# The last norm of a two-layer graph kernel: one-hot rows made on GpSimd by comparison, and one of a batch's four row loads issued by ScalarE

## The reference

```python
x = layernorm(x + gnn_0(x, ...))      # sums over edges, then four dense layers with tanh
x = layernorm(x + gnn_1(x, ...))      # one message of 32 features per edge, added at its destination
# layernorm(v) = (v - mean(v)) / sqrt(var(v) + 1e-5), over the 32 features of a node
```

## Time and profile before

| | |
|---|---|
| median of 3 runs | 1985.52 us |
| lowest, highest | 1982.97, 1986.45 us |
| span of the profiled execution (first to last instruction) | 1707.1 us |
| median less span (time outside the first and last instruction) | 278.4 us |
| VectorE, ScalarE, GpSimd, TensorE busy over the span | 70%, 50%, 63%, 77% |
| the last norm: from 1555.8 us to the last store's issue at 1699.4 us | 143.6 us, 8.4% of the span |
| mean granted TensorE clock over the span | 0.846 |

### The profile page before, as it was taken

One profiled execution on the slowest core, in us unless ns is written; L12 is line 12 of the kernel. 1 busy time (PEld: TensorE's weight loads), 2 busy tenths in 40 slices (PEclk: granted clock), 3 DMA queues, 4 the chain that ended last, 5 costly groups with the idle time before them and its releaser, 6 DMA issues.

```text
span 1707.1 us, 25367 instructions
## 1 busy us (share of the span) xinstructions
PE 1315.9 (77%) x6200; PEld 957.6 (56%) x6200; DVE 1193.5 (70%) x3648; ACT 858.9 (50%) x2256; POOL 1068.9 (63%) x1168
## 2 busy tenths in 40 slices
PE   5699993686513777665778999958999999996673
PEld 1388881242212555554655666635777777775563
DVE  9699995677512443676667999964777777774776
ACT  0167770011101222666775777735666666664884
POOL 7777778777777777774111444448877887830444
PEclk8599996577555999888888999977999999997655
DMA  1000000123224988665555666531222222213785
GB/s 41 13 14 13 14 14 20 47 72 79 67 68 127 257 250 246 171 174 145 132 138 140 179 184 189 163 95 32 58 58 57 58 64 67 59 42 78 196 216 157
DMA packets 298498, 178.98 MB, mean 105 GB/s; under 512 B 28715, under 2 KB 290032, under 8 KB 298352
## 3 DMA queue, kind: packets, MB, share of 16 engines
q1 hardware_dynamic: 219712, 116.54, 26.0%
q0 software_dynamic: 29008, 36.18, 8.3%
q10 hardware_dynamic: 49632, 24.65, 5.0%
HBM read 111.18 MB, written 66.07 MB: 104 GB/s over the span
## 4 chain that ended last, share of the span: by engine, by line
PE 42%; POOL 28%; issue 16%; DVE 8%; DMA 2%; DVEq 2%; SPq 1%; ACT 1%; POOLq 0%; ACTq 0%
PE bank L1025 12%; POOL gat L511 12%; POOL lined L518 11%; PE bank L994 7%; PE bank L1018 7%; DVE res L1308 5%; PE bank L945 3%; POOL out L591 3%; PE bank L947 3%; PE bank L1034 3%; PE bank L1003 3%; PE bank L987 3%; DMA placed<-pay,pos_i 1%; DVEq L1308 1%; DVEq L1302 1%
## 5 line engine op out<-in xcount | busy, mean ns | idle before, releaser
L566 POOL DMA_INDIRECT gat<-x_d,src_i x196 | 253.2, 1292 | 59.0 <-issue 53.1
L511 POOL DMA_INDIRECT gat<-in_x,key_i x196 | 211.1, 1077 | 64.8 <-issue 62.4
L1308 DVE TENSOR_TENSOR res<-res,bank 128x128 f32 x588 | 168.4, 286 | 108.5 <-issue 24.4
L528 POOL DMA_INDIRECT placed<-pay,pos_i x196 | 191.9, 979 | 68.1 <-issue 65.6
L518 POOL DMA_INDIRECT lined<-in_x,other_i x196 | 195.8, 999 | 59.7 <-issue 59.7
L1025 PE MATMUL bank<-prod,ident 128*128 128x280 f32 x896 | 217.0, 400 | 0.0
L1025 PEld LDWEIGHTS bank<-prod,ident 128*128 128x128 f32 x896 | 171.0, 191 | 46.5 <-issue 0.6
L956 PE MATMUL bank<-woh,pw 128*128 128x128 f32 x784 | 135.4, 335 | 69.3 <-DVE woh L1287 33.4
L956 PEld LDWEIGHTS bank<-woh,pw 128*128 128x128 f32 x784 | 120.3, 238 | 85.5 <-DVE woh L1287 44.5
L56 ACT ACTIVATE xt<-bank 128x128 f32<-128x128 f32 x98 | 26.6, 271 | 269.6 <-PE bank L897 261.2
L1018 PE MATMUL bank<-rw,ht 65*128 65x384 f32 x392 | 141.3, 514 | 23.3 <-ACT ht L738 13.8
(11 more groups left out here) (204 smaller groups left out, 2840.5 us busy)
## 6 DMA issues: line engine op xcount, KB each, us to landing
pw<-placed SPq DMA_DIRECT2D x588, 68.0 KB, 2.1
pw<-placed SPq DMA_DIRECT2D x98, 272.0 KB
xin<-in_x_t SPq DMA_DIRECT2D x53, 256.0 KB, 3.2
placed<-pay SPq DMA_DIRECT2D x49, 272.0 KB, 2.4
x_d<-res POOLq DMA_DIRECT2D x49, 256.0 KB, 3.8
placed<-pay SPq DMA_DIRECT2D x28, 448.0 KB, 3.2
out<-out ACTq DMA_DIRECT2D x49, 256.0 KB, 2.7
xin<-in_x_t ACTq DMA_DIRECT2D x45, 256.0 KB, 3.6
```

Source lines behind the costliest of these rows:

```text
L511: pool.indirect_dma_start(gat[:, t, :], None, x, bass.IndirectOffsetOnAxis(ap=key_i[:, 0, t:t + 1], axis=0)).then_inc(s_gat, 16)
L528: pool.indirect_dma_start(placed[1].rearrange("t p r -> (t p) r"), bass.IndirectOffsetOnAxis(ap=pos_i[:, 1, t:t + 1], axis=0), pay[i % 4][ ...
L566: pool.indirect_dma_start(gat1[g % 3][:, k, :], None, x1_d, bass.IndirectOffsetOnAxis(ap=src_i[:, t:t + 1], axis=0)).then_inc(c_gat[g % 3] ...
L1308: add.up(dve.tensor_tensor(into, into, quarter(bank + k // G, k % G), ALU.add))
```

## The change

GpSimd no longer subtracts; it makes the one-hot rows itself, with four `tensor_scalar` instructions per batch on 128x128: (iota + 128 * window) compared for equality with the row's key, the key read from column 128 of the loaded rows as a scalar per partition. Nothing goes over ScalarE any more: `away4`, its semaphore, the four 128x128 and the one 128x512 activation per batch are gone. On GpSimd the step is scale(s - 10), hot(s).

ScalarE's step is store(s - 13), square(s - 7), load(s): it now issues the fourth row load of each batch, with the register load for its tile number, and waits with it as SyncE does (`z_mm`, b - 5). SyncE issues the other three. ScalarE's first load also waits for a new semaphore `z_stored`, which SyncE raises when the stores of stage 3 are done. TensorE's and VectorE's lists are unchanged.

```diff
+BY_SP = 3
...
-        away4 = ring(sb, "away4", 2, [P, G, P])
...
-        def first_rows(sp, to, c, b, landed):
+        def first_rows(eng, on, to, c, b, ks, landed):
             _, tiles = nc.values_load_multi_w_load_instructions(
-                t0_i[0:1, c, G * b:G * b + G], engines=[mybir.EngineType.SP], min_val=0, max_val=NT,
+                t0_i[0:1, c, G * b + ks.start:G * b + ks.stop], engines=[on], min_val=0, max_val=NT,
                 skip_runtime_bounds_check_because=IN_RANGE)
-            for k in range(G):
-                sp.dma_start(to[:, k, :], placed[c][bass.ds(tiles[k], 1)].rearrange("t p r -> p (t r)")).then_inc(landed, 16)
+            for k, tile in zip(ks, tiles):
+                eng.dma_start(to[:, k, :], placed[c][bass.ds(tile, 1)].rearrange("t p r -> p (t r)")).then_inc(landed, 16)
...
             sp.wait_ge(c_mm, NU)
+            sp.sem_inc(z_stored, 1)
             for b in range(NB):
                 wait(sp, z_mm, b - 5)
-                first_rows(sp, pw4[b % 6], 1, b, z_pw[b % 6])
+                first_rows(sp, mybir.EngineType.SP, pw4[b % 6], 1, b, range(BY_SP), z_pw[b % 6])
...
-            def apart_4(b):
+            def hot_4(b):
                 pool.wait_ge(z_pw[b % 6], 16 * G * (b // 6 + 1))
-                wait(pool, z_away, b - 2)
-                pool.tensor_tensor(kr4[b % 3][:, :], w128[:, G * b:G * b + G], pw4[b % 6][:, :, P], ALU.subtract).then_inc(z_kr, 1)
-            staged([apart_4] + [None] * 9 + [scale_4], NB)
+                wait(pool, z_mm, b - 2)
+                for k in range(G):
+                    ins = pool.tensor_scalar(oh4[b % 3][:, k, :], iota[:, 0:P], float(P * (G * b + k)), pw4[b % 6][:, k, P:P + 1],
+                                             ALU.add, ALU.is_equal)
+                ins.then_inc(z_oh, 1)
+            staged([hot_4] + [None] * 9 + [scale_4], NB)
...
             act.wait_ge(c_mm, NU)
-            def away_from_4(b):
-                act.wait_ge(z_kr, b + 1)
-                wait(act, z_oh, b - 1)
-                for k in range(G):
-                    ins = act.activation(away4[b % 2][:, k, :], iota[:, 0:P], ACT.Abs, bias=kr4[b % 3][:, k:k + 1])
-                ins.then_inc(z_away, 1)
-            def hot_4(b):
-                act.wait_ge(z_away, b + 1)
-                wait(act, z_mm, b - 2)
-                act.activation(oh4[b % 3][:, :, :], away4[b % 2][:, :, :], ACT.Relu, bias=1.0, scale=-1.0).then_inc(z_oh, 1)
-            staged([away_from_4, hot_4, None, None, None, square_4] + [None] * 5 + [store_4], NB)
+            act.wait_ge(z_stored, 1)
+            def load_4(b):
+                wait(act, z_mm, b - 5)
+                first_rows(act, mybir.EngineType.Activation, pw4[b % 6], 1, b, range(BY_SP, G), z_pw[b % 6])
+            staged([load_4] + [None] * 6 + [square_4] + [None] * 5 + [store_4], NB)
```

More of the change, by code:

```diff
@@ L291, in gnn_kernel @@
         c_prod, c_sum, c_scal, c_pay, c_mm, c_msg = sem("c_prod"), sem("c_sum"), sem("c_scal"), sem("c_pay"), sem("c_mm"), sem("c_msg")
-        z_pw, z_kr, z_away, z_oh, z_mm = ring(sem, "z_pw", 6), sem("z_kr"), sem("z_away"), sem("z_oh"), sem("z_mm")
+        z_pw, z_kr, z_oh, z_mm, z_stored = ring(sem, "z_pw", 6), sem("z_kr"), sem("z_oh"), sem("z_mm"), sem("z_stored")
         z_y, z_sq, z_ssq, z_root, z_out = sem("z_y"), sem("z_sq"), sem("z_ssq"), sem("z_root"), sem("z_out")
@@ L446, in _ @@
                 freed(sp, b - 5)
-                first_rows(sp, pw[b % 6], 0, b, s_pw[b % 6])
+                first_rows(sp, mybir.EngineType.SP, pw[b % 6], 0, b, range(G), s_pw[b % 6])
             def load_extra(i, c):
@@ L463, in _ @@
                 wait(sp, s_back, min(i - 5 - D_EXTRA, NG))
-                first_rows(sp, pw[i % 6], 1, b, s_pw[i % 6])
+                first_rows(sp, mybir.EngineType.SP, pw[i % 6], 1, b, range(G), s_pw[i % 6])
                 if b >= 5:
```

## The result

The changed kernel takes 2049.5 us (2048.2 to 2053.2) where the one before takes 1986.0: ratio 1.0327, 95% interval 1.0304 to 1.0349, or 63.5 us slower. The prediction was 1995.3 with a range of 1970 to 2034: the right sign, and under a sixth of the size.

The account below looks back on a forecast made before the run. SyncE's loads were taken to bound the last norm at 2.54 us a batch, ScalarE close behind. Start -0.5, first nine intervals -4.1, other 39 +15.3 and tail -0.9 made +9.8 on 1985.5: 1995.3 us, range 1970 to 2034.

Parts of the forecast that it names:

- What binds before: Last norm: SyncE's loads lead at 2.40 us a batch plus hiccups, ScalarE second, 2.28 us busy a batch.
- the 15 us that were to show the forecast: Sign on GpSimd: its waits for loaded rows fall from 98.8 us to under 15.
- The comparison on GpSimd: GpSimd, last norm: a comparison costs between 0.25 and 0.60 us, taken as 0.40, four a batch; the deciding term.
- Rival C: GpSimd, last norm: comparison 0.60 us, 3.73 a batch, 2030 us, with the full lock 2045; chance 0.17.
- The first batches: First nine intervals of the last norm, without scale: TensorE leads at 2.08 us against 2.54, a gain of 4.1 us.
- The 0.5 us booked for an earlier first batch: Start of the last norm: the last of four loads is issued 0.5 us earlier, -0.5 us.
- The lock: VectorE's newton steps and GpSimd's operations shut each other out: 11 x 0.09 = 1.0 us of GpSimd in four batches.
- 0.4 and more: Sign on VectorE: newton steps lengthen from 0.23 us to 0.4 and more.
- SyncE at 1.88 us: SyncE, last norm: with one load fewer its batch takes 1.88 us and it no longer leads.
- rival B: GpSimd, last norm: comparison costs a one-input pass, 0.25 us; 2.33 a batch, 1971.8 us; chance 0.29.
- ScalarE's load hidden by three steps, and the gate: ScalarE's load goes out three GpSimd steps, over 7 us, ahead, so is hidden; the gate `z_stored` costs nothing measurable.
- Time outside the span: Whole kernel: 278.4 us lie outside the profiled span of 1707.1 us and are taken as they are.

Follow-up runs that it names:

- load_four_regs: load_only with SyncE reading four tile numbers into registers again and using three: 1691.3 us beside 1706.2 for the kernel before, ratio 0.9908.
- prices: The kernel before with each kind of GpSimd operation run alone at the very end, twelve times on 128x128, six on 128x512; two-operation comparison 0.707 us.
- oh_only: The changed kernel with all four loads back on SyncE, so only the comparisons on GpSimd: 2053.7 us beside 1991.6 for the kernel before, ratio 1.0290.
- load_only: The kernel before, its activations kept, with ScalarE issuing the fourth load of each batch: ratio 0.9998 to the kernel before.
- b_again: The kernel before, unchanged, profiled again: span 1990.7 us, ratio 0.9996.
- spread: The changed kernel's one-hot rows shared out, one by GpSimd, one by VectorE, two by ScalarE; three loads on SyncE, one on ScalarE: ratio 0.9998 to the kernel before.
- half_store: One GpSimd comparison a batch, three rows by ScalarE, loads split three and one, only two of four windows stored: ratio 0.9957 to the kernel before.
- two_two: load_only with two loads issued by SyncE and two by ScalarE: ratio 1.0059, 10.3 us over the kernel before.
- before: The first profile of the unchanged kernel before: span 1707.1 us, where its timed runs have a median of 1985.5.

## Why the prediction was wrong, step by step

- *What binds before.* Right: SyncE's loads, with ScalarE close behind. `load_four_regs` shows the first: relieve SyncE truly, and the batch falls to 2.25 us. ScalarE is then busy 95% of the time, which fits the second. One reading was off: 34.2 of GpSimd's 98.8 us of waiting stand before the first batch, so the wait could never fall under the 15 us that were to show the forecast; it fell to those 34.3.
- *The comparison on GpSimd.* This step failed. "Between 0.25 and 0.60; I take 0.40" was measured at 0.70 from one to the next in the steady part. I bounded an operation that the trace didn't hold by rows of other operations, products and copies, and put the dear end at a row that was dear for another reason. Rival C, with a chance of 0.17, had the mechanism that GpSimd leads by a dear comparison, but its price of 0.60 was too low as well, and its reason, an operation in two parts, is 0.12 of the 0.707 (`prices`). In the sum the term is 16 x 0.40 = 6.4 us in four batches; it should be 16 x 0.70 = 11.2, or 1.2 us a batch, 47 us on 39 batches of the 53.7 that were missing.
- *The first batches.* I had TensorE leading at 2.08 us; at 0.78 from one comparison to the next GpSimd led from the start, 31.3 us for ten batches, 3.13 each. Where a gain of 4.1 us was booked there came a loss of 5.3. The 0.5 us booked for an earlier first batch did not come either: from the last message matmul's start to the first comparison there are 4.7 us, as before to the first subtraction.
- *The lock.* Mostly wrong. GpSimd loses nothing to speak of (0.01 a step against 0.09), and VectorE's steps, which were each to wait for the rest of a comparison, run beside comparisons at 0.19 to 0.37 us; only the few beside a product lengthen, to 1.1. That the "0.4 and more" did not come is seen in line 1344's median of 0.226. The term overstated GpSimd's loss by 0.22 us a batch and, by luck, hid a part of the first error: with 0.70 and my other terms the batch is 4.13, measured 3.93.
- *SyncE at 1.88 us.* Wrong: the register load, taken at 0.30 us, had a median of 0.98 in the changed kernel, where four values have 0.60 (`oh_only`). In this kernel it was without effect, as GpSimd led. By `load_only`'s 2.48 us a batch it would have taken most of rival B's gain away even with a cheap comparison; no run shows that case itself.
- *ScalarE's load hidden by three steps, and the gate.* Right: no wait for rows after the first, `oh_only` and the changed kernel alike. The tail from the last comparisons' start to the last store is 2038.6 - 2020.75 = 17.9 us, 0.5 more than before where 0.9 less were forecast, as four comparisons take 2.8 us and not 1.6.
- *The rule on one-input operations.* Named for rival B: the Trainium skill (GPSIMD Engine Reference, section "Engine selection") has them at about line rate and two-input ones some two times slower than VectorE. Here the one-input comparison costs 3.3 ns a column and the two-input product 1.63. On 128x128 the copy (0.283) and add with multiply (0.288) cost less than the two-input product (0.443), as by the rule; the lone add (0.518) and every comparison (0.516 to 0.707) cost more. There the measurement decides.
- *Time outside the span.* Wrong, as told above. It did no harm to a difference of two sums over the last norm.

The sum with measured terms: nine intervals x (3.13 - 2.54) = 5.3, 39 x (3.93 - 2.54) = 54.2, tail 0.5: 60.0 us, of 60.4 between the profiles and 63.5 between the medians; the 3 us between these two are not accounted for.

## What to carry to other kernels

Where a change puts an operation on an engine on which the trace has never shown it, the nearest rows of other operations don't bound it: on GpSimd, one instruction with different operations lay between 0.29 and 0.71 us on one shape. Price it alone in one run first, and count against the batch of the engine that receives it. When a step is made shorter, look at every instruction of its queue afterwards, register loads too: here a count of three values instead of four took back nearly all that the missing DMA issue gave, and reading four again turned a neutral change into a gain of 0.9%.

## What the runs showed of the hardware that I had not expected

- In the median a register load of four values takes 0.30 us on SyncE (`b_again`, `load_four_regs`) but 0.60 in `oh_only`, of three 0.67 (`spread`, `half_store`) to 0.98 (changed kernel), of two 0.91 on SyncE and 0.99 on ScalarE (`two_two`), of one 0.28 (changed kernel) to 0.45 (`load_only`) on ScalarE.
- GpSimd's tensor-scalar instructions on 128x128 float32: add with multiply by constants 0.288, a lone add 0.518, a comparison with a constant 0.516, with a scalar per partition 0.591, that behind an add 0.707 (`prices`).
- VectorE waits out GpSimd's 128x512 product, 0.75 to 1.11 us for a step of 0.2, but runs beside GpSimd's comparison at 0.19 to 0.37 (changed kernel); its own 128x128 comparison takes 0.27 to 0.39 us away from a product and 0.69 to 1.09 beside one (`spread`).
- In the sorting stage, while GpSimd issues gathers, the same program has TensorE busy 87.7 of 90 us in one profile (`before`) and 18.2 in another (`b_again`); the kernel before takes 1704 to 1707 us in three groups of runs and 1986 to 1992 in two. What makes the difference was not tried.
